# Mamba block with a mixture of experts on one core: front stages placed earlier, expert tile ahead of the projections, tile rows first on the DMA queue

## The reference

```python
xz = xn @ W_in.T; u, z = split(xz)                  # 512 + 512 channels
u = silu(causal_conv4(u) + conv_b)
dt, B, C = split(u @ W_xp.T, [16, 32])              # 16, 16, 16 columns
dt = softplus(dt @ W_dt.T + b_dt); A = -exp(A_log)  # 16 states per channel
h_t = exp(dt_t * A) * h_{t-1} + dt_t * u_t * B_t    # scan over 1024 tokens
y = (sum_n h_t * C_t + u * D) * silu(z)
x = x + xn0 + y @ W_out.T
...
logits = xf @ router_w + router_b; top 2, softmax over the two
out = x + sum_k w_k * (silu(xf @ gate_k) * (xf @ up_k)) @ down_k
```

## Time and profile before

| what | us |
| --- | --- |
| median of 3 runs | 3042.28 |
| lowest and highest | 3037.51, 3044.11 |
| profiled execution, its own time | 3046.68 |
| its span in the trace | 3044.9 |
| TensorE clock granted, mean | 0.817 of full speed |

### The profile page before, as it was taken

One profiled execution on the slowest core, in us unless ns is written; L12 is line 12 of the kernel. 1 busy time (PEld: TensorE's weight loads), 2 busy tenths in 40 slices (PEclk: granted clock), 3 DMA queues, 4 the chain that ended last, 5 costly groups with the idle time before them and its releaser, 6 DMA issues.

```text
span 3044.9 us, 34043 instructions
## 1 busy us (share of the span) xinstructions
PE 1986.4 (65%) x8672; PEld 1105.0 (36%) x8672; DVE 2249.9 (74%) x3168; ACT 1533.8 (50%) x2414; POOL 2113.2 (69%) x1499
## 2 busy tenths in 40 slices
PE   4465665786747685586846867487764868556564
PEld 1112131444315351254414443154522535144453
DVE  0498988887868688787877878687887878789322
ACT  2565746465544655456454565446544564534111
POOL 0697869767696678867697676967688666976312
PEclk9687877798868897798867988688977989668888
DMA  3533343667457764566637574567736766375576
GB/s 122 141 91 96 95 114 84 179 169 187 110 158 184 183 185 113 163 185 177 159 112 197 155 202 116 149 177 189 190 99 169 191 163 173 110 200 158 163 213 193
DMA packets 271490, 473.01 MB, mean 155 GB/s; under 512 B 36928, under 2 KB 114752, under 8 KB 271168
## 3 DMA queue, kind: packets, MB, share of 16 engines
q1 hardware_dynamic: 259008, 437.26, 53.6%
q0 software_dynamic: 12288, 33.57, 3.5%
HBM read 372.38 MB, written 98.30 MB: 155 GB/s over the span
## 4 chain that ended last, share of the span: by engine, by line
POOL 32%; issue 17%; DVE 15%; PE 14%; DMA 9%; SPq 6%; ACT 6%; POOLq 0%; DVEq 0%; ACTq 0%
POOL hs L979 16%; DMA xt<-sorted_x 6%; DVE dA L778 5%; POOL sorted_x L1007 4%; PE p_g L553 4%; DVE hs L778 3%; POOL hs L990 3%; POOL pair L1017 2%; POOL dtb L998 2%; POOL dtub L996 2%; PE ring L443 2%; PE ring L435 2%; SPq L341 2%; DMA out<-xr 1%; PE p_a L534 1%
## 5 line engine op out<-in xcount | busy, mean ns | idle before, releaser
L979 POOL TENSOR_TENSOR hs<-rep_dtu,b_bc 128x1024 f32<-128x1024 f32 x512 | 1195.8, 2360 | 24.1 <-DMA rep_dtu<-dt_d 14.3
L697 ACT ACTIVATE dA<-rep_dt,a_s 128x512 f32<-128x512 f32 x1024 | 675.8, 684 | 616.3 <-DVE hs L789 453.7
L523 PE MATMUL yps<-hs,const_s 128*32 128x512 f32 x2048 | 335.0, 730 | 361.6 <-POOL hs L990 327.0
L990 POOL TENSOR_TENSOR hs<-hs,c_bc 128x512 f32<-128x512 f32 x256 | 330.5, 1291 | 343.9 <-DVE hs L778 333.0
L778 DVE TENSOR_TENSOR_SCAN dA<-dA,hs 128x512 f32<-128x512 f32 x384 | 453.5, 1211 | 56.1 <-POOL hs L979 46.7
L778 DVE TENSOR_TENSOR_SCAN dA<-dA,carry,hs 128x512 f32<-128x512 f32 x384 | 476.6, 1272 | 14.8 <-POOL hs L979 11.7
L553 PE MATMUL p_g<-xy,w_e 128*128 128x128 f32 x2944 | 424.1, 306 | 41.5 <-DVE hT L888 41.4
L553 PEld LDWEIGHTS p_g<-xy,w_e 128*128 128x128 f32 x2944 | 414.7, 223 | 75.2 <-issue 72.3
L435 PE MATMUL ring<-xnT,w_in_s 128*128 128x512 f32 x512 | 329.8, 778 | 104.3 <-ACT sz L634 64.3
L789 DVE TENSOR_TENSOR hs<-dA,c_bc 128x1024 f32<-128x1024 f32 x256 | 312.1, 1219 | 4.4
L885 DVE SCALAR_TENSOR_TENSOR th<-th,p_g 128x256 f32<-128x256 f32 x184 | 76.5, 416 | 312.1 <-ACT th L718 312.0
(11 more groups left out here) (113 smaller groups left out, 2805.1 us busy)
## 6 DMA issues: line engine op xcount, KB each, us to landing
w_e<-in_w_moe SPq DMA_DIRECT2D x184, 512.0 KB
rep_dt<-dt_d SPq DMA_DIRECT2D x256, 256.0 KB
rep_dtu<-dt_d SPq DMA_DIRECT2D x256, 256.0 KB, 8.7
w_e<-in_w_moe SPq DMA_DIRECT2D x184, 256.0 KB
xt<-sorted_x SPq DMA_DIRECT2D x184, 128.0 KB
sorted_y<-xy SPq DMA_DIRECT2D x184, 128.0 KB
dt_d<-dtb SPq DMA_DIRECT2D x32, 512.0 KB
dt_d<-dtub SPq DMA_DIRECT2D x32, 512.0 KB
```

What stands on the lines that cost most here:

```text
L523: last = pe.matmul(yps[32 * j:32 * j + 32, :], sumsel, hs[:, u % 3, j, :], start=False, stop=g == G - 1, skip_group_check=True)
L697: act.activation(dA[:, j, :], rep_dt[:, c % 2, j, :], ACT.Exp, scale=a_s[:, n, j:j + 1]).then_inc(s_exp, 1)
L979: pool.tensor_tensor(hs[:, u % 3, a:a + 2], rep_dtu[:, c % 2, a:a + 2], b_bc[:, g, :].unsqueeze(1).to_broadcast([P, 2, T]), ALU.mult).then ...
L990: pool.tensor_tensor(hs[:, u % 3, 3], hs[:, u % 3, 3], c_bc[:, g, :], ALU.mult).then_inc(s_hp, 1)
```

## The change

- Ring items have one table, PLACES, by slot from the block's first unit. The front starts three slots earlier (X0 at -19 instead of -16) and its items are spread anew; the tail keeps O, F and R, and K0 moves from 22 to 23.
- In a slot PE and ACT do the expert tile first, then all ring items (ACT: the decay of part 2 between tanh and the items).
- SP puts the rows of the next tile and the tile's store at the head of a slot and the weights at its end; dt stores, the copies for chunk 0 and 1, and the load of x are placed anew.
- `dtu` is split: `smooth` (L996, L998) at n = 8 and 12, `dtu` (L1001) at n = 9 and 13. `norm_x`, `deviation` and `moments` of the block after the next move to n = 12, 11 and 10.
- Scatter starts one slot later; gathers of a group are at every second slot, from n = 11 of an even block on (every slot for the last group). The combine comes two slots after its gather, its store three slots after.
- On DVE, `round_off`, `route`, `place`, `weights` and `combine` stand ahead of the scans of parts 3 and 2. `route` is at n = 6, `place` at n = 8.
- The router bias is added by a matmul of ones; the logits are evicted as they are; one instruction compares both best indices of all tokens, in place of a cast and eight compares.

```diff
-FIRST = -UN - 3
-SCATTER = 7
-LG, PL = 5, 8
+FIRST = -UN - 7
+SCATTER = 8
+LG, PL = 3, 8
...
-        self.gather = self.start + STAGES + 1
+        step = 2 if per == 1 else 1
+        self.gather = {k: self.start + STAGES + 1 + step * k for k in range(NT)}
...
-FRONT_RING = {0: ["X0", "X1", "U0"], 3: ["W0"], 4: ["U1"], 5: ["W1"], 6: ["U2", "U3"], 7: ["W2"], 8: ["W3"], 9: ["P0"],
-              10: ["D0", "D1"], 11: ["Z0", "Z1"], 12: ["Z2"], 13: ["Z3"], 14: ["D2", "D3"]}
-TAIL_RING = {1: ["O0"], 2: ["O1"], 4: ["F0", "F1"], 5: ["R0"], 6: ["K0"]}
+PLACES = {-19: ["X0", "X1", "U0"], -18: ["U1"], -17: ["W0"], -16: ["W1"], -13: ["U2", "U3"], -12: ["W2"], -11: ["W3"],
+          -10: ["P0"], -9: ["D0", "D1"], -8: ["Z0"], -6: ["Z1"], -5: ["D2", "D3"], -4: ["Z2", "Z3"],
+          17: ["O0"], 18: ["O1"], 20: ["F0", "F1"], 21: ["R0"], 23: ["K0"]}
+SMOOTH = {8: 0, 12: 1}
...
# SP, in a slot
+                for g, at in moe_at(s):
+                    if 0 <= at + 1 < NK:
+                        load_tile(g, at + 1)
+                    if 0 <= at - 4 < NK:
+                        store_tile(g, at - 4)
+                for g, i in gathered(s - 3):
+                    store_out(g, i)
+                for g, i in gathered(s - 1):
+                    load_xr(g, i)
+                if 0 <= q < NQ and n in (0, 4, 8):
                     load_rep(q, n // G + 1)
...
+                if front and n == 7:
                     store_bc(q + 1)
+                if front and n in (10, 14):
+                    store_dt(q + 1, int(n == 14))
                 if front and n == 12:
-                    store_dt(q + 1, 0)
-                if front and n == 13:
                     load_rep(q + 1, 0)
...
                     if 0 <= at - 1 < NK:
                         load_down(g, at - 1)
                     if 0 <= at + 1 < NK:
-                        load_tile(g, at + 1)
+                        load_expert(g, at + 1)
...
# PE, in a slot
-                items = ring_in(s)
-                for item in items[:1]:
-                    through_ring(item)
                 for g, at in moe_at(s):
                     if 0 <= at - 3 < NK:
                         down(g, at - 3)
                     if 0 <= at < NK:
                         tile_transpose(g, at)
-                for item in items[1:2]:
-                    through_ring(item)
-                for g, at in moe_at(s):
                     if 0 <= at - 1 < NK:
                         gate_up(g, at - 1)
-                for item in items[2:]:
+                for item in ring_in(s):
                     through_ring(item)
...
# DVE: the router's compare, and the order in a slot
-                then(dve.tensor_copy(ixf[:], ix[:, :, 0:2]))
-                for i in range(QT):
-                    for k in range(2):
-                        last = dve.tensor_scalar(hot[:, k, at + i, :], iota, ixf[:, i, k:k + 1], None, ALU.is_equal)
-                then(last)
+                then(dve.tensor_tensor(hot[:, 0:2, at:at + QT], ix[:, :, 0:2].rearrange("p i k -> p k i").unsqueeze(3).to_broadcast([P, 2, QT, NE]),
+                                       iota.unsqueeze(1).unsqueeze(1).to_broadcast([P, 2, QT, NE]), ALU.is_equal))
...
+                if n in SMOOTH and 0 <= q + 1 < NQ:
+                    round_off(2 * (q + 1) + SMOOTH[n])
+                if tail and n == 6:
+                    route(q - 1)
+                for g in ALL:
+                    if s == g.scatter[0]:
+                        place(g)
+                    if s == g.scatter[0] + 1:
+                        weights(g)
+                for g, i in gathered(s - 2):
+                    combine(g, i)
                 if unit:
                     unit_last(s)
...
# POOL
-                if n in (11, 15) and 0 <= q + 1 < NQ:
-                    dtu(q + 1, int(n == 15))
+                if n in SMOOTH and 0 <= q + 1 < NQ:
+                    smooth(q + 1, SMOOTH[n])
+                if n - 1 in SMOOTH and 0 <= q + 1 < NQ:
+                    dtu(q + 1, SMOOTH[n - 1])
```

More of the change, by code:

```diff
@@ L919, in _ @@
                     moments(1, q - 1)
-                if tail and n == 5:
-                    route(q - 1)
-                for g in ALL:
-                    if s == g.scatter[0] - 1:
-                        place(g)
-                    if s == g.scatter[0] + 1:
-                        weights(g)
-                if n == 13 and 0 <= q + 2 < NQ:
+                if n == 10 and 0 <= q + 2 < NQ:
                     moments(0, q + 2)
-                for g, i in gathered(s - 1):
-                    combine(g, i)
         @block.gpsimd
@@ L990, in weigh, with smooth @@
                 pool.tensor_tensor(hs[:, u % 3, 3], hs[:, u % 3, 3], c_bc[:, g, :], ALU.mult).then_inc(s_hp, 1)
-            def dtu(q, h):
+            def smooth(q, h):
                 v = 2 * q + h
```

61 lines of the change are left out of this document (21 added, 40 removed).

## The result

The changed kernel takes 3142.41 us (median of 4 runs, 3140.34 to 3147.2) against 3042.82 for the kernel before on the same chip. The ratio is 1.0333, with a 95% interval of 1.0315 to 1.0351: 100 us slower, where I forecast 102 us faster. It lies outside my range. The profiled execution took 3140.5 us, with a span of 3138.7.

The account below looks back on a forecast made before the run. Waits bound the kernel: POOL's stretch, then DVE waiting for ACT's tanh. Five full pairs -75, blocks 2 and 3 -22, 14 and 15 -2, 0 and 1 +1, start +10, tail -15: total -103, 2940 us, range 2845 to 3080.

Parts of the forecast that it names:

- the sum of waits in Part 2: DVE's waits in odd n = 2 to 15 and even n = 0 to 6: about 41 us to 35, -6 per pair.
- Part 2, n = 4 to 6: Norm of x2, F, W, R, silu, P0 serial through one ring bank: 31 us for three slots against 33 and about 39.
- Part 2, O0 and O1: Out-projections behind the tile at n = 1, 2: residual waits 3 us each, loss per pair 10 us against about 1.
- rival (d): Ring items late on PE at a low clock, ACT waiting in order ahead of decays: slower, 3135; chance 0.17.
- Part 2, n = 11 to 14: Softplus, silu, norm_x and X, U0 pile on ACT: waits of 12.7 us in an odd pass against 13 to 14.
- Part 3: Router and order on DVE: router 5.8 us becomes about 2, -7.6 a pair; combine loses half, 8 a pair, +5 back.
- rival (e): DVE work newly ahead of the scan is blocked at the port by POOL's L979: 3135, or about 3075; chance 0.1.
- Part 1: Next tile's rows first on SP, weights last: 7.8 us landing covered, worth nothing to 9.7 us per odd pass.
- Part 4: Gathers spread, scatter later, smooth split: POOL's stretch 125.6 us against 134, -8 per pair, bounds 0 and -13.
- Part 5: The ends: start about +10 us, blocks 0 and 1 together +1, tail -15 with bounds 0 and -25.
- (b): ACT's pile at n = 11 to 14 and 4 to 6 mostly hidden: 13 us more per pair, 2860; chance 0.2.
- (c): Waits only change place and POOL's stretch gives nothing: 3035 to 3050; chance 0.08.

Follow-up runs that it names:

- experiment 13: The changed kernel with only the front stages' places put back as before; 2980.14 us, ratio 0.978.
- experiment 15: Experiment 9 with convolutions U2, U3, W2 and W3 moved early, to n = 0 to 3; 2949.82 us, ratio 0.9692.
- Experiment 1: The changed kernel with out-projections O0 and O1 again ahead of the expert tile on PE; 3030.45 us, ratio 0.9962.
- Experiment 4: The kernel before with only the expert tile put ahead of all ring items on PE and ACT; 3165.89 us, ratio 1.0402.
- experiment 7: The kernel before with only rows and tile store at the head of SP's slot, weights at the end; 2995.49 us, ratio 0.9865.
- experiment 12: Experiment 8 with all front items at the places of before; 2878.35 us, ratio 0.9459.
- experiment 16: Experiment 9 with Z1 to Z3 and their silu moved ahead of D2 and D3, to n = 9 and 10; 2942.71 us, ratio 0.9665.
- experiment 9: Experiment 8 with block 1's front also put behind the first scan; 2970.73 us, ratio 0.9765.
- experiment 8: Experiment 1 with DVE's round_off, route, place, weights and combine behind the scans again; 2991.54 us, ratio 0.9852.
- experiment 10: Experiment 1 with only round_off put back behind the scans on DVE; 3007.33 us, ratio 0.9881.
- experiments 7, 3: The second of the two: the changed kernel with SP's list in the order of before; 3245.29 us, ratio 1.0668.
- experiment 11: Experiment 8 with a gather in every slot again, eight in a row; 3073.23 us, ratio 1.0091.

## Why the prediction was wrong, by its own steps

**The step that failed: the sum of waits in Part 2.** I wrote for odd n = 2 to 15 and even n = 0 to 6: "about 41 us now, 35 after: -6 per pair". I took DVE's waits in these slots from both traces, with an instruction put in the slot whose L789 (L781) it follows, as a mean of the five full pairs. They are 40.2 us before, so my 41 was right, and 55.8 after. By items, and for experiment 13, which is the change with the places of before:

| slots | waits before | after | experiment 13 |
| --- | --- | --- | --- |
| even n = 1, 2 and odd n = 2 (O0, O1) | 2.3 | 17.5 | 18.3 |
| n = 4 to 6 (norm of x2, F, W2, R, W3, silu) | 9.4 | 22.4 | 8.9 |
| odd n = 7, 8 | 2.1 | 2.5 | 0.4 |
| odd n = 11 to 15 | 19.0 | 13.4 | 7.1 |
| the others | 7.3 | 0.0 | 2.6 |

The waits for the tanh went as meant. What I had too low is what came in their place at two points: the out-projection for the residual, and the convolutions at n = 4 to 6. The same slots are 11.6 us longer in a pair, where Parts 2 and 3 gave -8.6.

**Part 2, n = 4 to 6: the term that was wrong outright.** I forecast 31 us for the three slots against 33 and 39, 62 a pair against 72. They take 73.3, and 59.6 in experiment 13: the other parts of the change do bring the gain, and the new places take it back. 19.8 of the 22.4 us are late decays. I took the waits of ACT for W2 and W3 for short ones. But W2 starts on PE only when F1 has left the one bank, and W3 behind R0; ACT, which takes in order, stands 5.54 us for each with the next decays behind it (timeline at experiment 15). The eight records of W2 take 5.76 us in the mean of these ten passes, against 3.70 at n = 7 before and 3.65 in experiment 13.

**Part 2, O0 and O1: right mechanism, term too small.** I wrote "Loss per pair 10 us against about 1 now", 9 net. Experiment 1 measured 112 in all, and 16.8 in each full pair. Two things were missing. A wait is about 5 us, not 3: the gate matmuls (1.95 to 3.27) and the out-projection (3.62) run wholly after DVE's gate. And the out-projection now stands behind the tile's rows, so that late rows reach the residual, 7.58 us at odd n = 2. Experiment 4 has this loss in the kernel before, beside that of the router. My sign for rival (d) was "L815 waits over 6 us" and scans that wait for ACT: 7 of the 25 waits are over 6, six of them at odd n = 2, and the scans do wait.

**Part 2, n = 11 to 14: sized about right.** I had waits of 12.7 us in an odd pass "against 13 to 14 now"; odd n = 11 to 15 have 13.4 after and 19.0 before. The row silu, norm and X costs by itself: with the places of before the same slots have 7.1, and are 50.9 us long in place of 54.6. I let the new pile and the old wait of the earlier trace rows cancel, and the old one would have shrunk anyhow, if not gone: with rows first alone (experiment 7) these slots have 14.2.

**What the places cost.** They are 162 us in the change (experiment 13) and 113 in the kernel with the other faults cured (experiment 12). Of the 113, the silu in the pile is 28 (experiment 16), the convolutions beside norm of x2 are 21 (15) and the start is 21 (9 against 8), each undone on its own. The other 43 I have not split; the three were not tried together.

**n = 7, D0 and D1:** `round_off` waits 26 times for 158.5 us in place of twice for 93.2. The first two of the 26, ahead of the scan, are 88.2 (68.92 and 19.23), so that the other 24 are 70 us that were not there before; I had a gain of 3 a pass.

**Part 3, the router's cost.** Right: the subtraction takes 0.166 us in the median (1.841 before), in 16 executions, with the longest at 1.818. By the Trainium skill, page "SBUF — State Buffer", section "Who interferes with whom", a DVE instruction with two SBUF inputs contends with a GpSimd instruction that reads SBUF. The trace agrees: the 15 long ones before, and the three after that take over 1 us, start while POOL is in its drive multiply (L979, L966) and end 0.02 to 0.03 us behind it; the short ones have none beside them. The one-instruction compare takes 0.225 us in the mean (L826), about the value I chose. The combine did not lose half: L882 has a mean of 0.987 (1.151 before), but its second half, L884, has 0.824 (0.532 before); together 1.81 against 1.68. Behind the scans, as in experiment 8, the two are 2.28.

**Part 3, the order on DVE: wrong sign.** I gave it gains, and `round_off` its own waits (2.6 and 2.7), but no price for who stands behind them. Experiment 8: the order costs 39 us, although it saves DVE 71 us of work, and 23 of the 39 are `round_off` (experiment 10). The reading is that it waits for ACT's softplus while the scan of part 3 stands behind it, and POOL's weigh, ACT's decays and the next drive all stand behind that scan; with the extras last, DVE's wait for the drive falls from 192.3 to 138.1 us, that for decays does not fall (256.5 and 280.9). The mechanism of rival (e) was the port. The loss came in the same place, ahead of the scan, but out of a wait.

**Part 1, rows first: right, and much too small.** I folded it into the tanh waits (-6 a pair in all). It is worth 44 us alone and, with the combine's transfers, 103 inside the change (experiments 7, 3). The tanh wait in the odd stretch, forecast at under 8 us, is not in the list of that stretch at all. "PE's wait for the tile's rows is nearly gone" did not hold: it is 101.3 us, from 220.9.

**Part 4, the gathers.** I had n = 7 of an even to n = 1 of an odd block at 125.6 us against 134, -8 a pair. The 134 has no row behind it: taken like the 177.3, from L789 to L789, these eleven slots are 128.1 us before and 128.7 after, so the gain is nothing. Even n = 7 to odd n = 0 lose 3.5 us, and odd n = 1 takes them back. DVE's waits in the POOL stretch did move as written, none for pairs now and POOL's drive instead (waits of DVE from 1581 to 1697):

```profile
DVE dA L770 <- POOL hs L966: 29.5, 8, 6.4
```

The spreading by itself is worth more than I gave it, 82 us in experiment 11. So in the change this gain is there and something in the same slots eats it: `round_off` waits 4.4 us at n = 8 of the even block, and n = 1 of the odd block (9.0 to 13.6) waits 4.0 for the combine's x rows.

**Part 5.** Start: +20 measured, +10 forecast. ACT stands idle 9.2 us there for ring items that go one by one through the one bank, most of it for the four in-projection records of U0 and of U1, 3.75 and 3.78 us a group; my +10 had too little for them. Blocks 0 and 1: +22 against +1. Block 1's early front is not the reason, since they are no shorter with it behind the first scan (experiment 9: 287.3 us against 284.4 in experiment 8); with the places of before they are 266.6 (experiment 13), so it is the places within the blocks. Blocks 2 and 3: +5 against -22. Tail: -20 against -15, about right.

**The rivals.** (b) gave the pile as mostly hidden, and it is not. (c) had the right picture, waits that only change place, but no price for a new wait that is larger than the old. (d) had about the right time and, for n = 4 to 6, the mechanism: ACT stands in its order for ring items that are late on PE, ahead of decays. Its price was the matmul rate, about 2 us an item at the low level. For the out-projection that is not so (0.387 us a record, 0.402 before). For W2 it is a part: 5.76 in place of 3.70 us, and the granted clock from 1556 to 1573 is 0.83; no run parts the rate from the late start. (e) had about the right time and the wrong cause. The case that came true was a sum: a gain of 100 us and more by Parts 1 and 4, against some 112 for the out-projection, 39 for DVE's order and 113 to 162 for the places. These do not add, since a cured wait often bares another.

## What to carry to other kernels

When one edit changes the order in a slot and the slots too, do not compare a group of slots with the old trace alone: ask what it would take with the other parts of the edit in. Here n = 4 to 6 stand at 73.3 us after 72.3 and look unchanged, and only the run with the places of before (59.6) shows what they cost. Work that one engine makes and another takes in order must be looked at for what stands behind the taker, here decays. A consumer with an early due time (here the residual) must be looked at by itself when the order of its producer's list changes; whatever its producer newly stands behind, late transfers too, is now its own lateness. And before work that waits is moved ahead of a scan or a decay on an in-order engine, list who waits for that scan: here 23 us went by one instruction that used to wait where nobody stood behind it.

## What was not expected of the hardware

One bank that is handed between two in-order engines, which also make each other's inputs, ties their lists together. Putting the first item of every slot ahead of the tile in PE's list alone, and not the out-projections only, costs 147 us against experiment 1 (3177.01 against 3030.45), with ACT waiting 342.0 us for the tiles' transposes behind a blocked item. And eight gathers in a row, with their combines, go with late plain loads: the x rows of the combine came late 21 times for 119.5 us in experiment 11, and 8 times for 37.7 in experiment 8, with a wait of 27.7 in each. Whether the transfers or the order of SP's list make them late was not taken apart.
